# A two-layer conditioned attention kernel: one written-out order for all 32 batches, a PSUM bank for each batch, statistics in two slots, and row maxima transposed by a DMA

## The reference, cut to what matters

```python
# layer 0: linear attention, 8 heads of 32
xn = ln(x) ; q = softmax(xn@Wq+bq, within a head) ; k = softmax(xn@Wk+bk+mask, over tokens) ; v = (xn@Wv+bv)*mask
att = einsum('bnhd,bnhl->bhdl', k, v) ; y = einsum('bnhd,bhdl->bnhl', q, att)
h = silu(ln(y)*(1+scale)+shift) @ W_out + b_out ; x = x + h     # scale, shift from silu(cond) @ W_emb + b_emb
# layer 1: full attention, 16 heads of 16
xn = ln(x) ; att = softmax(q k^T + mask, over the second token) ; y = att @ v
x = x + silu(ln(y)*(1+scale)+shift) @ out_w + out_b
```

## Time and profile before

| | before |
|---|---|
| median of 3 runs | 960.46 us (955.67 to 961.33) |
| profiled execution | 959.34 us, of which the span is 957.5 us |
| PE, DVE busy | 852.1 us (89%), 821.8 us (86%) |
| ACT, POOL busy | 698.3 us (73%), 739.6 us (77%) |
| mean granted TensorE clock | 0.953 |

### The profile page before, as it was taken

The page is one execution under the profiler, slowest core; times in us unless marked ns, Lnnn a source line. Parts: engine busy times, 40 slices in busy tenths (PEclk is TensorE's granted clock), DMA queues, the critical chain, the costliest instruction groups (busy, mean ns, idle before and its releaser), DMA issues.

```text
span 957.5 us, 25672 instructions
## 1 busy us (share of the span) xinstructions
PE 852.1 (89%) x8715; PEld 614.1 (64%) x8715; DVE 821.8 (86%) x1678; ACT 698.3 (73%) x1236; POOL 739.6 (77%) x1212
## 2 busy tenths in 40 slices
PE   3866688899999999999999999999999998888774
PEld 1755576566777777777777777777777775554432
DVE  7869859899999999999999999999999998777732
ACT  0222364588888888888888888888888888778763
POOL 9345898788988888889888888888888877765221
PEclk9577899899999999999999999999999999999977
DMA  7111143434444544344434434343334332333100
GB/s 206 23 30 38 36 101 90 92 92 93 91 103 102 103 87 103 97 99 103 103 98 90 98 98 102 91 91 90 96 103 103 103 81 81 81 101 103 39 25 33
DMA packets 140090, 83.76 MB, mean 87 GB/s; under 512 B 78262, under 2 KB 132636, under 8 KB 139964
## 3 DMA queue, kind: packets, MB, share of 16 engines
q1 hardware_dynamic: 139964, 82.13, 35.7%
HBM read 39.52 MB, written 25.79 MB: 68 GB/s over the span
## 4 chain that ended last, share of the span: by engine, by line
DVE 38%; PE 33%; issue 17%; POOL 9%; ACT 1%; SPq 1%; DMA 1%; DVEq 0%; POOLq 0%; ACTq 0%
PE banks L696 10%; DVE NM L1061 10%; DVE st L962 6%; PE banks L683 4%; PE banks L664 4%; POOL XB L1777 4%; PE banks L607 3%; PE banks L541 3%; PE banks L618 3%; DVE wemb L1101 2%; DVE Y L1085 2%; DVE V L1003 2%; DVE V1t L1053 2%; DVE qm L992 2%; DVE km L976 2%
## 5 line engine op out<-in xcount | busy, mean ns | idle before, releaser
L1061 DVE TENSOR_REDUCE NM<-banks 128x4 f32<-128x1024 f32 x256 | 304.0, 1216 | 28.0 <-PE banks L664 25.4
L1582 ACT ACTIVATE wraw<-banks,uu 128x1024 f32<-128x1024 f32 x154 | 170.4, 1117 | 32.5 <-PE banks L683 31.7
L1754 POOL TENSOR_TENSOR SH<-ST,SH 128x512 f16<-128x512 f32 x64 | 84.5, 1320 | 52.5 <-ACT SH L1550 52.5
L1582 ACT ACTIVATE PX<-banks,uu 128x1024 f32<-128x1024 f32 x102 | 113.1, 1116 | 14.7 <-PE banks L683 14.2
L664 PE MATMUL banks<-SK,SQ 51*128 51x256 f16 x1024 | 100.5, 273 | 24.1 <-DVE V L1003 11.1
L541 PE MATMUL banks<-wo,SH 128*128 128x256 f16 x768 | 96.6, 284 | 14.5 <-POOL SH L1754 13.4
L683 PE MATMUL banks<-SQ,SK 53*128 53x256 f16 x1024 | 95.6, 274 | 6.2 <-DVE NM L1061 1.8
L541 PE MATMUL banks<-wv,ZT 128*128 128x256 f16 x768 | 98.5, 280 | 0.0
L1700 POOL TENSOR_TENSOR rs<-ve,nhalf 128x2 f32<-128x2 f32 x128 | 89.4, 698 | 10.6
L541 PEld LDWEIGHTS banks<-wo,SH 128*128 128x128 f16 x768 | 74.9, 101 | 33.0 <-POOL SH L1754 14.6
L696 PE MATMUL banks<-wraw,V 128*32 128x256 f32 x1232 | 88.6, 388 | 3.0 <-ACT wraw L1582 2.1
(11 more groups left out here) (186 smaller groups left out, 2012.8 us busy)
## 6 DMA issues: line engine op xcount, KB each, us to landing
scr<-AB SPq DMA_DIRECT2D x64, 256.0 KB, 3.0
...
```

The lines of the kernel that those rows point to most:

```text
L1061: V.tensor_reduce(NMe[:, c, :, 2 * g:2 * g + 2], banks[:, n:n + 2, :].rearrange("p a (h m) -> p a h m", m=T), AX.X, ALU.max, negate=True). ...
L1582: A.activation(px(v % 5), banks[:, n:n + 2, :].rearrange("p a n -> p (a n)"), ACT.Exp, scale=uu[:, 0:1]).then_inc(S["exp"])
L1754: G.tensor_tensor(SH[:, l, 1], ST[:, l], SH[:, l, 0], ALU.subtract).then_inc(S[f"sl{l}"])
```

## The change

The computation stays the same. Four things are different.

1. The loop of 47 rounds is replaced on all five streams by a list of calls for all 32 batches and for the setup. The lists differ from batch to batch.
2. `BANK` gives each piece a bank for each batch (a string of 32 digits), and `FREED` names for each piece and batch the one or two steps after which the bank is free.
3. `mv`, `nm` and `rs` have two slots, by the parity of the batch; waits on the step of the batch before become waits on that of the batch before that one. Waits on the own semaphore of the same engine are added (`s{l}`, `r{l}`, `z{i}`).
4. `ntT` and `nt` are gone, and with them `identb`. `NT` is filled from `NMw` by a DMA transpose `nT(b)` on SP.

The core of the diff:

```diff
 BANK = {
-    "gk0": 3, "gkt": 3, "gq0": 2, "gqt": 7, "gv0": 5, "gat": 1, "gy0": 5, "gy0T": 0,
+    "gk0": "27251067011624154630233461074070",
...
+FREED = {
+    "gty1": (
+        "max:22 max:26 yt:12 yt:16 yt:20 yt:24 yt:28 yt:32 yt:36 yt:40 yt:45 Y1:23 at:20 yt:57 yt:60 yt:64 "
...
-        mv = sb("mv", [P, 4, 2, 2])
+        mv = sb("mv", [P, 2, 4, 2, 2])
...
-        NT = sb("NT", [32, T], F16)
+        NT = sb("NT", [P, 2, P], F16)
...
         def clear(e, g, b):
+            for before in FREED[g].split()[b].split("+"):
+                name, _, n = before.partition(":")
+                if n:
+                    e.wait_ge(S[name], int(n))
+                elif name != "-":
+                    ready(e, name)
...
+            def nT(b):
+
+                e.wait_ge(S["np"], b + 1)
+                if b >= 1:
+                    e.wait_ge(d_nw[(b - 1) % 2], 16 * ((b - 1) // 2 + 1))
+                e.dma_start(NT[:, :, :], NMw[:, :, :].rearrange("p c n -> p (c n)"), transpose=True).then_inc(d_nt[b % 2], 16)
...
-                e.wait_ge(S["nt"], b + 1)
+                e.wait_ge(d_nt[o], 16 * (b // 2 + 1))
...
-            def ntT(b):
-                e.wait_ge(S["np"], b + 1)
-                clear(e, "gnt", b)
-                nt = banks[:, BANK["gnt"], 0:P].bitcast(F16)
-                for c in range(2):
-                    m = PE.transpose(nt[:, c * P:(c + 1) * P], NMw[:, c, :], identb[:, :])
-                m.then_inc(S["ntT"])
...
             def stats(b, l, src):
+                e.wait_ge(S[f"s{l}"], b)
...
             def s0(b):
                 e.wait_ge(d_x[b % 3], 16 * (b // 3 + 1))
-                e.wait_ge(S["r0"], b)
+                e.wait_ge(S["r0"], up(b - 1))
...
             def norm(b, l):
+                e.wait_ge(S[f"r{l}"], b)
...
             def r0(b):
                 e.wait_ge(S["s0"], b + 1)
-                e.wait_ge(S["z0"], b)
+                e.wait_ge(S["z0"], up(b - 1))
...
-            for i in range(ITERATIONS):
-                if i == 0:
-                    ld_m()
...
+            x_in(0); x_in(1); x_in(2); ld_m(); ld_c(); ld_w0(); ld_w1(); ld_r(); ld_o1(); ld_o0(); ld_f1(); mbd0()
+            ld_f0(); am(0); am(1); am(2); z0T(0); aug_d(); z0T(1); x_in(3); am(3); x_in(4); z0T(2); am(4); am(5)
```

More of the change, by code:

```diff
@@ new lines @@
+    "gty1": "27645330516302132131000401223100",
+    "gy1T": "36442523362510215230030000260320",
+    "go1": "67272406060032634344751122330600",
+    "gpm": "0",
+    "grow3": "1",
+    "gcnd": "0",
+    "gcol": "5",
+    "grow0": "3",
+    "gbb0": "3",
+    "grow1": "2",
+    "gbb1": "2",
+    "grow2": "4",
+    "gbb2": "1",
+    "gt_w0": "4",
+    "ga_w0": "0",
+    "gt_w1": "3",
+    "ga_w1": "3",
+    "gt_o0": "1",
+    "ga_o0": "1",
+    "gt_o1": "3",
+    "ga_o1": "4",
+    "gt_f0": "0",
@@ L105 @@
     "PE": (
-        "pm tr_w0 ar_w0 row1 row0 row3 col cnd bb1 tr_w1 fm0 ar_w1 tr_o1 bb0 tr_b tr_o0 ar_o1 ar_o0 tr_f0 "
-        "row2 ar_f0 fm1 ar_b bb2 tr_f1 ar_f1 ").split(),
+        "pm row3 row1 row0 cnd tr_w0 bb0 ar_w0 row2 bb1 col fm0 tr_o0 tr_w1 tr_f0 tr_o1 ar_f0 ar_o1 ar_o0 "
+        "ar_w1 tr_b fm1 ar_b tr_f1 bb2 ar_f1 ").split(),
     "DVE": (
-        "mb0 w0m mx_w0 perm w0p fr1 csl w1m bm mc csT p3 wl_q0 mx_w1 wl_v0 wl_k0 o1m bc1 fr0 w1p bc0 o0m "
-        "mx_o1 f0m o1p mx_b mx_o0 mx_f0 wl_o1 o0p fr2 film0 f1m fcs wl_o0 mb1 wl_v1 wl_k1 wl_q1 mx_f1 bc2 "
-        "film1 ").split(),
+        "mb0 csl mc w0m fr0 csT mx_w0 fr1 perm bc1 o0m w0p p3 bm wl_v0 wl_k0 o1m fr2 wl_q0 bc0 w1m f0m mx_w1 "
+        "mx_f0 mx_o1 mx_o0 w1p mx_b o0p wl_k1 film0 wl_o0 f1m wl_v1 wl_q1 fcs mb1 mx_f1 o1p wl_o1 bc2 film1 ").split(),
     "ACT": (
-        "th wh_v0 wh_k0 wh_q0 wh_q1 wh_o1 wh_k1 wh_o0 wh_v1 ").split(),
+        "th wh_v0 wh_q0 wh_k0 wh_k1 wh_q1 wh_o0 wh_v1 wh_o1 ").split(),
     "POOL": (
-        "cst fill nmz v1z ").split(),
+        "nmz cst fill v1z ").split(),
 }
-ITERATIONS = NB + 15
 PIECES = (
     "s0 r0 z0 xb0 k0 km ke ktT kt rk q0 q1 qm qs qe qtT qt rq v0 v att at y0 Y0 s1 r1 yn0 y0T th0 st0 sh0 "
-    "sl0 o0 x1 s2 r2 z1 xb1 q1p qa spq k1p ka spk v1p vt vm rows max np ntT nt cols exp pv yt ty Y1 s3 r3 "
+    "sl0 o0 x1 s2 r2 z1 xb1 q1p qa spq k1p ka spk v1p vt vm rows max np cols exp pv yt ty Y1 s3 r3 "
     "yn1 y1T th1 st1 sh1 sl1 o1 o").split()
@@ L158, in bass_cond_seq @@
         d_mk = [sem(f"d_mk{i}") for i in range(3)]
+        d_nt = [sem(f"d_nt{i}") for i in range(2)]
         d_nw = [sem(f"d_nw{i}") for i in range(2)]
@@ L566, in k0 @@
                     e.wait_ge(l_aug, 48)
[L567 removed]
+                zt, w, dst = ZT[:, b % 2, 0], W["k", 0], bank(home("gk0", b))
                 for f in range(2):
@@ new lines, in _ @@
+            cols(25, 0); pv(24, 6); pv(24, 7); cols(25, 1); rows(26, 4); v1p(27); ty(24, 1); rows(26, 5)
+            cols(25, 2); rows(26, 6); pv(25, 0); pv(25, 1); k1p(28); rows(26, 7); cols(25, 3); o1(23); q1p(28)
+            cols(25, 4); o0(29); y0T(30); y0(31); cols(25, 5); pv(25, 2); pv(25, 3); rows(27, 0); pv(25, 4)
+            y1T(24); v1p(28); rows(27, 1); pv(25, 5); cols(25, 6); cols(25, 7); ty(25, 0); rows(27, 2)
+            rows(27, 3); pv(25, 6); pv(25, 7); rows(27, 4); rows(27, 5); o0(30); cols(26, 0); ty(25, 1)
@@ L975, in km @@
                 e.wait_ge(S["ke"], b)
-                follow(V.tensor_reduce(kmx[:, :], bank(BANK["gk0"]), AX.X, ALU.max, negate=True))
+                follow(V.tensor_reduce(kmx[:, :], bank(home("gk0", b)), AX.X, ALU.max, negate=True))
                 V.tensor_scalar(kmx[:, :], kmx[:, :], un[:, 1:2], None, ALU.mult).then_inc(S["km"])
@@ L1106, in largest @@
                 k = AR[x]
-                follow(V.tensor_reduce(mxc[0:n, k:k + 1], banks[0:n, BANK[f"gt_{x}"], 0:P], AX.X, ALU.max))
+                follow(V.tensor_reduce(mxc[0:n, k:k + 1], banks[0:n, home(f"gt_{x}"), 0:P], AX.X, ALU.max))
                 V.tensor_scalar(mxd[0:n, 3 * k:3 * k + n], ident[0:n, 0:n], mxc[0:n, k:k + 1], None, ALU.mult).then_inc(C["DVE"])
@@ L1685, in _ @@
+            sh1(30); th1(31); sh1(31)
         @block.gpsimd
```

906 lines of the change are left out of this document (493 added, 413 removed), and 187 rows, old and new, of tables (BANK, FREED, HELD).

## The result

| | before | after |
|---|---|---|
| median | 960.35 us (4 runs, 955.67 to 961.33) | 921.44 us (4 runs, 920.96 to 923.43) |
| profiled execution | 959.34 us, span 957.5 | 921.15 us, span 919.4 |

The ratio is 0.9608, with a 95% interval of 0.9574 to 0.9642: the change makes the kernel 39 us faster. A second series of five runs of the same kernel gave 923.69 us and a ratio of 0.9613 (0.9596 to 0.9631). The forecast of 930 us was 8.6 us too high, and its range of 910 to 956 held the time.

The account below looks back on a forecast made before the run. The prediction took TensorE, busy 98.3%, to set the period in the middle, with engines waiting elsewhere. Its terms +2 - 19 - 2 - 5 - 5 = -29 took 959.3 us to 930, range 910 to 956.

Parts of the forecast that it names:

- Up to the first `km`: First 45.2 us: more early vector work falls under `fill`; ends 0 and +5 us, taken as +2.
- one more wait like the 4.89: Start: upper end of +5 us, after a small vector copy that took 4.89 us while `fill` ran.
- First `km` to first `max`: Stage of 102.4 us: 74 us of VectorE work plus 9 idle makes 83, a gain of 19.
- two slots that let `s0` and `r0` run ahead: First `km` to first `max`: with early norms, addresses GpSimd's 33.6 us of waits; part of the gain of 19.
- To batch 10: Stage from 147.6 to 250.1 us: calls close to the old sequence; at most 8 us, taken as a gain of 2.
- The middle: 21 periods of 25.03 us: TensorE sets the period; ends -15 and +15 us, taken as a gain of 5.
- the floor of 24.33: Middle: lowest period in us, 25.03 less 0.28 for the transposes and 0.42 for the gap, worth 15 us.
- The path of the maxima: Maxima to `cols` by DMA transpose: extra time hidden by SP's delay, else up to 0.9 us a period; taken as nothing.
- The tail: After the middle: ScalarE waits less in the 136.4 us, ends 0 and -14, taken -5; last 45.3 us nothing or +1.
- The start does not shorten: Rival, chance 0.12: `fill` and the vector work behind it set the pace, the start's net 17 us are lost, 947 us.
- The maxima come late: Rival, chance 0.14: `cols` starts about 1 us late in the 21 periods and the ramps around them, 954 us.
- TensorE starves behind ScalarE: Rival, chance 0.10: second `ty` waits for its copy `yt`, 1.7 us a period, 36 us over the middle, 971 us.

Follow-up runs that it names:

- e9: Kernel after, with the third batch's first norm moved later, no longer right behind the first two: 928.31 us, ratio to before 0.9661.
- e6: Kernel after, with the waits of before, so the second slot of the statistics is unused: 923.60 us, ratio to before 0.9617.
- e2: Kernel after, with `fill` written by ScalarE instead of GpSimd: 904.97 us, again 906.16 us, ratios to before 0.9430 and 0.9431.
- e5: Kernel before, with only the DMA transpose of the maxima replacing TensorE's two transposes and VectorE's copy: 960.37 us, ratio to before 0.9997.
- e7: Kernel after, with two more 128x128 transposes per batch on TensorE: 925.43 us, ratio to before 0.9639.
- e8: Kernel after, with the DMA transpose of the maxima issued twice in series: 928.17 us, ratio to before 0.9666.

## Why the prediction was right, and where it was not

By stage the forecast missed by +8.7, -7.9, -5.9, -3.4, +0.6 and -1.2 us. The first of these hides the second, and to that extent it is luck that the total came so near.

**Up to the first `km`, forecast +2, measured +10.7.** The step saw the mechanism, early vector work falling under `fill`, and put its size wrong: "one more wait like the 4.89" as the upper end. There were four waits where there had been three, and above all they came one behind the other from 6.5 to 26.8 with nothing else done between. `fill` ended at 26.7 us, even earlier than the 28.4 that the step took, but by then VectorE had done only `mb0`, where before it had done `w0m`, `perm` and more. The right term was the vector work that still stood behind `fill`, 29.4 us from 26.7 to the first `km`. By the runs with `fill` on ScalarE the collision costs 18.6 us in after and 8.3 in before.

**First `km` to first `max`, forecast -19, measured -26.9.** Half of the mechanism held: GpSimd's wait for statistics fell from 33.6 to 12.1, and one early norm alone is worth 4.5 us (e9). The other half, two slots that let `s0` and `r0` run ahead, is worth nothing (e6). The size was off on both terms: VectorE has 69.1 us of work there and not 74, and idle time of 6.4 and not 9. The busy 77.2 us that the step began with were not all work: 3.7 of them were the operation of `mb1` held by `v1z`, which also lengthened GpSimd's waits. As the border between the two stages moved, only their sum means much: -16.2, forecast -17. It was near because two misses cancelled. Without the collision the first `max` came at 114.9 (e2), which is -32.7.

**To batch 10, forecast -2, measured -7.9.** The step took the busy 94.4 us of VectorE as a floor near 94 and then trusted a likeness of the sequences. VectorE is busy 84.7 us after and TensorE 86.8: the stage holds less work (160 vector instructions for 183, 876 matmuls for 926), since more was done ahead of it, and idle time of the busier engine went from 8.1 to 7.8. A part of this difference is work that moved over the border, not time that an order saved. Another part is the granted clock, which the step names and does not price: 0.95 in before, where it was 0.92 up to 170 us and 0.83 from there to 190, and 1.00 in after. The two executions of e2 differ by 3.0 us at 0.96 and 1.00, so an estimate is some 3 us of the 7.9. The runs do not separate the parts, and do not show what made the clock differ.

**The middle, forecast -5, measured -8.4.** Near in number and wrong in its reason. "TensorE sets the period" was read from 98.3% busy time, and the floor of 24.33 was made of 0.28 for the transposes and 0.42 for the gap. The transposes alone gave 0.0 (e5): the period of before was a ring over VectorE, GpSimd and TensorE. The gain belongs to the new order and banks (which of them is open), and only because they break that ring does TensorE's time count at all (e7), the transposes' share of it included. By the ratio of e7, their 2.7 us would be worth about 1.8 us in after: an estimate from the two runs. The one-line view of the chain shows it in the kernel before already, with TensorE at 31.1%; the step argues from busy time, timeline and waits and does not use it. The Trainium skill warns of the same number for another reason, in "Perfetto Trace Analysis", "Identifying the Most-Contended Engine": matmul busy time is not a good measure of how close TensorE is to its limit, because matmuls are pipelined. This case agrees with the warning, 98.3% busy in before with 2.7 us less work for no gain, but the reason that the runs show is the ring.

**The path of the maxima.** Right to be taken at nothing. In after the transpose is issued at 518.75 and lands 2.3 us later (2.5 to 3.1 were taken), and the write of what it made goes out only at 523.76, behind three other transfers. No matmul in the middle of after waits for a DMA, and one weight load does, for 0.4 us.

**The tail, forecast -5, measured -4.4 and -1.2.** Near in number, but no run tests its reason.

**The rivals.** "The start does not shorten" had its condition half right: `fill` and the vector work behind it did set the pace, and the early norms still paid. "The maxima come late" did not happen, and even one more hop costs TensorE only the waits shown (e8). "TensorE starves behind ScalarE" did not happen: in the middle no matmul waits for ScalarE for more than 0.4 us.

**The faster version.** `fill` on ScalarE takes the kernel from 921 to 924 us down to 905 or 906, ratio to before 0.943 (0.9415 to 0.9445), and is the version to keep.
